# One full transpose a block for the router's scores, two normalisations and two joins moved to GpSimd, the last waits moved to SyncE

## What is computed

```python
n = layernorm(x)
s = sigmoid(silu(n @ s_w1.T + s_b1) @ s_w2.T + s_b2)
u = (n @ B_w.T + B_b) * s                  # 128 numbers a row
h[t] = h[t-1] @ A.T + u[t]                 # along each sequence
y = h @ C_w.T + C_b + n @ D_w.T + D_b
x1 = x + y * sigmoid(n @ g_w.T + g_b)
```

```python
n = layernorm(x1)
chosen = argmax(n @ gate_w.T)              # 8 scores a row
out = x1 + n + n @ expert_w[chosen].T
```

## Time and profile before

| | |
|---|---|
| median of 3 runs | 916.51 us |
| profiled execution | 915.37 us, of which span 913.6 us |
| PE busy | 894.5 us, 98% |
| DVE busy | 674.2 us, 74% |
| ACT busy | 651.8 us, 71% |
| POOL busy | 403.2 us, 44% |
| granted TensorE clock, mean over the span | 0.995 of full |
| a steady block (blocks 2 to 14) | 41.0 us |
| DMA | 172.36 MB, mean 189 GB/s |

### The profile page before, as it was taken

How to read it: one execution, slowest core, us unless ns; L and a number is a source line. 1 busy time by engine, 2 the same in 40 slices (tenths; PEclk the granted TensorE clock), 3 DMA queues, 4 the chain that set the end, 5 groups by cost and what they waited for, 6 DMA issues and landing times. The chain is left out here.

```text
span 913.6 us, 15779 instructions
## 1 busy us (share of the span) xinstructions
PE 894.5 (98%) x4461; PEld 722.8 (79%) x4462; DVE 674.2 (74%) x1697; ACT 651.8 (71%) x878; POOL 403.2 (44%) x640
## 2 busy tenths in 40 slices
PE   8999999999999999999999999999999999999995
PEld 7777878787878878787878878787877887888884
DVE  6777878788887878788787888787786465555552
ACT  5578697978879797978879797978534445666661
POOL 1033536281735536181735537181523453443442
PEclk9999999999999999999999999999999999999998
DMA  8445395867768495867668495867889879988871
GB/s 315 132 92 142 90 220 127 200 149 190 153 165 205 96 218 131 198 149 192 154 159 208 98 215 136 199 144 174 296 273 413 340 249 252 217 221 211 199 188 37
DMA packets 231049, 172.36 MB, mean 189 GB/s; under 512 B 155701, under 2 KB 189237, under 8 KB 229952
## 3 DMA queue, kind: packets, MB, share of 16 engines
q1 hardware_dynamic: 220032, 137.71, 60.5%
q0 software_dynamic: 10800, 33.70, 11.0%
q10 hardware_dynamic: 144, 0.07, 0.0%
HBM read 81.63 MB, written 54.68 MB: 149 GB/s over the span
## 5 line engine op out<-in xcount | busy, mean ns | idle before, releaser
L1757 PE MATMUL y<-experts,x1T_hi 128*128 x568 | 180.5, 399 | 0.8 <-DVE x1T_lo L1402 0.8
L597 POOL TENSOR_SCALAR ln_var_eps<-ln_mean_var 128x4 f32<-128x4 f32 x16 | 3.6, 224 | 277.0 <-DVE ln_mean_var L1078 276.9
L652 POOL DMA_INDIRECT out<-gate,ids x71 | 72.6, 1022 | 111.1 <-DVE gate L1421 78.6
L1757 PEld LDWEIGHTS y<-experts,x1T_hi 128*128 128x128 f32 x568 | 103.2, 188 | 20.8 <-issue 1.1
L1757 PE MATMUL y<-experts,x1T_lo 128*128 x284 | 111.5, 392 | 0.0
L587 POOL TENSOR_TENSOR y_biased<-y_biased,gate 128x256 f32<-128x256 f32 x120 | 93.3, 799 | 25.6 <-DVE y_biased L1068 25.5
L1456 PE MATMUL gates<-GwT_hi,xT_hi 128*128 128x512 f32 x256 | 104.0, 406 | 0.0
L1456 PE MATMUL y<-DwT_hi,xT_hi 128*128 128x512 f32 x256 | 102.6, 401 | 0.5 <-DVE gateT L1000 0.5
L1458 PE MATMUL gates<-GwT_hi,xT_lo 128*128 128x512 f32 x256 | 100.5, 393 | 0.0
L1421 DVE TENSOR_TENSOR gate<-y,raw_weights 128x512 f32<-128x512 f32 x71 | 49.0, 691 | 69.4 <-PE y L1757 63.8
L1457 PE MATMUL gates<-GwT_lo,xT_hi 128*128 128x512 f32 x256 | 100.2, 391 | 0.0
(11 more groups left out here) (283 smaller groups left out, 2328.9 us busy)
## 6 DMA issues: line engine op xcount, KB each, us to landing
raw_weights<-routed_rows SPq DMA_DIRECT2D x71, 258.0 KB, 3.2
x_in<-L_attn_x SPq DMA_DIRECT2D x32, 512.0 KB, 4.2
x_rows<-L_attn_x SPq DMA_DIRECT2D x32, 512.0 KB, 5.1
turned_experts<-raw_weights SPq DMA_DIRECT2D x32, 512.0 KB, 3.6
experts<-turned_experts SPq DMA_DIRECT2D x8, 2048.0 KB, 14.6
raw_weights<-L_ffn_expert_w SPq DMA_DIRECT2D x32, 256.0 KB, 3.1
routed_rows<-padrow SPq DMA_DIRECT2D x9, 258.0 KB, 4.6
out<-gate,ids POOLq DMA_INDIRECT x71, 3.9
```

The lines of the kernel that those rows point to most:

```text
L652: nc.gpsimd.indirect_dma_start(out=out_rows, out_offset=bass.IndirectOffsetOnAxis(ap=ids[r][:, 0:1], axis=0), in_=res[r], in_offset=None, ...
L1757: ins = nc.tensor.matmul(Y[m % 2][:], x2T[a][:, k, m % 2 * P:(m % 2 + 1) * P], flat[:, bass.ds(first + (w * KD + k) * D, D)], start=(k == ...
```

## The change

**Scores.** The tile scoresT becomes [128, 128], filled with zeros once. ScalarE copies each of the four tiles' [16, 128] to its own 32 partitions (two copies a pair, of 128 columns). One transpose of the whole tile, once a block, replaces four of 16 rows; it stands where the second turn-back stood, and the first one is gone. VectorE's sum skips the unused columns. Because the first turn-back no longer waits for ScalarE's first copy, the second pair's first score product does. **GpSimd** normalises tiles 3 and 4 of the next block (normalise_late) and joins both expert pieces of blocks 1 to 14 (join_piece); ScalarE keeps tiles 1 and 2 and the pieces of blocks 0 and 15, and waits for GpSimd's. **SyncE** holds the final waits for the output stores, which GpSimd held.

```diff
-    SC_RANK, SC_COUNT, SC_TURN = 2 * NT * E, 3 * NT * E, 2 * P
+    QUAD = P // NT
+    SC_RANK, SC_COUNT, SC_TURN = P, P + NT * E, 2 * P
...
-        scT = kb("scoresT", [2 * E, 2 * P])
+        scT = kb("scoresT", [P, P])
...  (sync, at its end)
+            for r in range(R):
+                sp.wait_ge(out_sent[r], 16 * len(range(r, SLOTS, R)))
...  (gpsimd, constants)
+                    nc.gpsimd.memset(scT[:], 0.0),
...
-                wait(pool, S_["xn_ready"], NT * b)
+                if b > 0:
+                    pool.wait_ge(S_["xn_ready"], NT + NT // 2 * (b - 1))
+                    wait(pool, S_["xn_late"], NT // 2 * (b - 1))
...
+            def normalise_late(b, i):
+                pool.wait_ge(S_["shift1_ready"], b + 1)
+                nc.gpsimd.tensor_scalar(xin[:, i, :], xin[:, i, :], rs1[:, i:i + 1], shift1[:, i:i + 1],
+                                        ALU.mult, ALU.add).then_inc(S_["xn_late"], 1)
+            def join_piece(b, j):
+                pool.wait_ge(w_flip[j], 16 * (b + 1))
+                pool.wait_ge(w_low[j], b)
+                nc.gpsimd.tensor_copy(planes(w_whole[j].rearrange("p k t -> p (k t)")),
+                                      w_flipped[j].rearrange("p (h k) t -> p h (k t)", h=2)).then_inc(w_joined[j], 1)
...  (gpsimd body, after the identities, before rstd2)
+                if b < LASTB:
+                    normalise_late(b + 1, 2)
+                    normalise_late(b + 1, 3)
+                if 0 < b < LASTB:
+                    for j in range(2):
+                        join_piece(b, j)
...  (gpsimd, at its end)
-            for r in range(R):
-                pool.wait_ge(out_sent[r], 16 * len(range(r, SLOTS, R)))
...  (scalar, scoresT)
-                nc.scalar.activation(scT[:], score_bank(b)[0:2 * E, SC_TURN:], ACT.Copy).then_inc(S_["scoresT_ready"], 1)
+                for i in range(2):
+                    at = (2 * pair + i) * QUAD
+                    ins = nc.scalar.activation(scT[at:at + 2 * E, :], score_bank(b)[0:2 * E, SC_TURN + i * P:SC_TURN + (i + 1) * P],
+                                               ACT.Copy)
+                ins.then_inc(S_["scoresT_ready"], 1)
...  (scalar, halve)
-                normalise1(b, i)
-                act.wait_ge(S_["xn_ready"], NT * b + i + 1)
+                if i < NT // 2:
+                    normalise1(b, i)
+                    act.wait_ge(S_["xn_ready"], NT + NT // 2 * (b - 1) + i + 1)
+                else:
+                    act.wait_ge(S_["xn_late"], NT // 2 * (b - 2) + i + 1)
...  (scalar, join_piece: the join itself only if b in (0, LASTB))
...  (tensor, score_product)
                 if n == 0:
                     pe.wait_ge(S_["x2T_lo"], NT * b + 2 * pair + 2)
+                    if pair > 0:
+                        counted_waits(pe, (S_["scoresT_ready"], 2 * b + pair))
...
-            def tail_back(b, pair):
-                counted_waits(pe, (S_["scoresT_ready"], 2 * b + pair + 1))
-                for i in range(2):
-                    at = (2 * pair + i) * 2 * E
-                    ins = nc.tensor.transpose(score_bank(b)[:, at:at + 2 * E], scT[:, i * P:(i + 1) * P], ident[0:2 * E, 0:2 * E])
-                ins.then_inc(S_["scores_psum"], 1)
+            def tail_back(b):
+                counted_waits(pe, (S_["scoresT_ready"], 2 * b + 2))
+                nc.tensor.transpose(score_bank(b)[:, 0:P], scT[:], ident[:]).then_inc(S_["scores_psum"], 1)
```

More of the change, by code:

```diff
@@ L185, in preln_ssm_moe_kernel @@
                      "bias_sum w_turned w_hi w_lo pow_psum pow_copied pow_hi pow_lo "
-                     "gate_stats gate_mean gate_centred stats1 mv1_ready ve1_ready rstd1_ready neg1_ready shift1_ready xn_ready xT_psum x_halves joined xT_hi xT_lo "
+                     "gate_stats gate_mean gate_centred stats1 mv1_ready ve1_ready rstd1_ready neg1_ready shift1_ready xn_ready xn_late xT_psum x_halves joined xT_hi xT_lo "
                      "s1_psum s1_sig silu_ready silu_hi silu_lo bt_psum s2_psum sel_ready "
@@ L549, in _ @@
                     nc.gpsimd.memset(xrow[0][:, :, D:RW], 0.0), nc.gpsimd.memset(xrow[1][:, :, D:RW], 0.0),
-                    nc.gpsimd.memset(zeros[:], 0.0), nc.gpsimd.memset(onehot[:, NT, :], 0.0), nc.gpsimd.memset(taken[:], 0.0)]
+                    nc.gpsimd.memset(zeros[:], 0.0), nc.gpsimd.memset(scT[:], 0.0), nc.gpsimd.memset(onehot[:, NT, :], 0.0), nc.gpsimd.memset(taken[:], 0.0)]
             for ins in made:
@@ L759, in join_piece @@
             def join_piece(b, j):
-                act.wait_ge(w_flip[j], 16 * (b + 1))
-                wait(act, w_low[j], b)
-                nc.scalar.activation(planes(w_whole[j].rearrange("p k t -> p (k t)")),
-                                     w_flipped[j].rearrange("p (h k) t -> p h (k t)", h=2), ACT.Copy
-                                     ).then_inc(w_joined[j], 1)
+                if b in (0, LASTB):
+                    act.wait_ge(w_flip[j], 16 * (b + 1))
+                    wait(act, w_low[j], b)
+                    nc.scalar.activation(planes(w_whole[j].rearrange("p k t -> p (k t)")),
+                                         w_flipped[j].rearrange("p (h k) t -> p h (k t)", h=2), ACT.Copy
+                                         ).then_inc(w_joined[j], 1)
                 act.wait_ge(w_joined[j], b + 1)
@@ L1088, in choose @@
             def choose(b):
-                dve.wait_ge(S_["scores_psum"], 2 * b + 2)
-                nc.vector.tensor_reduce(scores[:], score_bank(b)[:, 0:SC_RANK].rearrange("p (t h e) -> p t e h", h=2, e=E),
+                dve.wait_ge(S_["scores_psum"], b + 1)
+                parts = score_bank(b)[:, 0:SC_RANK].rearrange("p (t q) -> p t q", q=QUAD)[:, :, 0:2 * E]
+                nc.vector.tensor_reduce(scores[:], parts.rearrange("p t (h e) -> p t e h", e=E),
                                         AX.X, ALU.add).then_inc(S_["scores_ready"], 1)
@@ L1695, in body @@
                 gates(b, 1, 0, 1)
-                if tail:
-                    tail_back(b - 1, 0)
                 if not by_dma(b - 1, NT - 1):
@@ L1706, in body @@
                     if tail:
-                        tail_back(b - 1, 1)
+                        tail_back(b - 1)
                     over(b, 5)
@@ L1785, in last_tail @@
                     tail_scores(LASTB, 0)
-                elif s == 10:
-                    tail_back(LASTB, 0)
                 elif s == 11:
@@ L1790, in last_tail @@
                 elif s == 13:
-                    tail_back(LASTB, 1)
+                    tail_back(LASTB)
                 elif s == 15:
```

## The result

| | us, median | range | runs |
|---|---|---|---|
| before | 916.26 | 915.50 to 917.07 | 4 |
| after | 964.76 | 963.81 to 965.63 | 4 |

The ratio is 1.0529, 95% interval 1.0513 to 1.0544: 48.5 us more, where 8.6 us less was forecast, far outside the range of 904 to 913. The profiled execution after took 963.81 us with a span of 962.0.

A forecast was written before the change was run, and what follows sets the result against it. The prediction took TensorE's queue, busy 894.5 of 913.6 us, as the bound. Savings of 4.3 and 4.4 us at the two turn-backs, less 0.1 for a memset, gave 8.6 us: 907.9 us, range 904.0 to 913.0.

The forecast's parts named there:

- Part 1, the turn-back: Scores on TensorE: one full transpose a block replaces four small ones; 4.3 us saved at the second turn-back, 4.4 at the first.
- rival 4: TensorE's stall before the turn-back belongs to its wait, not its 16 rows, and stays: 912.2 us; chance 0.09.
- give-back: New TensorE wait for VectorE's last subtraction at a scan step the first turn-back had covered: 13 x 0.18 = 2.3 us lost.
- covered as below: ScalarE's scores copy of 0.37 us becomes two, 0.5 us taken; said to be hidden by ScalarE's lighter load.
- part 2: Normalisations and joins move from ScalarE to GpSimd: 0.7 and 1.3 us each, 18 us of room there, no gain alone.
- So this alone gains nothing.: Taking normalisations and joins off ScalarE saves no time, since TensorE never waits for ScalarE in a steady block.
- Rival 1: GpSimd's joined piece is late, ScalarE waits and TensorE loses 1.0 us in each of 13 blocks: 921 us; chance 0.09.
- No cost: GpSimd's first joined piece is ready at 415.4 us, ScalarE goes on as before: moving the work costs nothing.
- VectorE gets in its way: VectorE's operations slow GpSimd's new normalising and joining: 1 us added to GpSimd's stretch.
- Rival 2: GpSimd's new work slows VectorE's scan chain, 13 x 4 x 0.3 = 15.6 us more: 924 us; chance 0.09.
- Part 3: Last waits for the output stores move to SyncE: gain up to about 1 us, cost up to 0.5; 0 taken.
- scan subtractions above 0.4 us beside GpSimd's new work: Named sign, in VectorE's scan steps, that the forecast is wrong because GpSimd's work slows VectorE.

The follow-up runs named there:

- e17_relief: Kernel before with the full transpose; GpSimd normalises one column of tiles 3 and 4, ScalarE none of them: 907.82 us, 0.9906 of before.
- e1_scores: Kernel after with only the full transpose left; normalising, joins and last waits as before: 916.25 us, 0.9991 of before.
- e4_two_input: Kernel before with full transpose and late normalisations on GpSimd, each as two operations with two tensor inputs; no joins there: 929.70 us, 1.0148 of before.
- e5_gaps: Kernel after, with GpSimd waiting for the end of each of its four new operations: 924.95 us, 1.0082 of before.
- e16_dose: Kernel before, with two added back-to-back GpSimd copies whose results nobody uses: 931.63 us, 1.0167 of before.

## Why the prediction was wrong, step by step

1. *What bounds the kernel.* Right: TensorE, and the two turn-backs as its largest repeated stall.
2. *Part 1, the turn-back.* Right in size: 0.12 us measured for the full transpose (0.15 taken), the drain gone (rival 4 falls), a give-back of 2.4 us (2.3 taken) at the step that was named, and 8.6 us in all in e17_relief. Its own range was added up a little low: a transpose of 0.11 to 0.23 us and a give-back of 1 to 4 us make 906.0 to 910.9, not 905.5 to 910.5. But its condition was missed. The two score copies (0.53 us; 0.5 taken) were called "covered as below", and the cover is part 2. Without it they cost the whole gain (e1_scores).
3. *"So this alone gains nothing."* Wrong for that reason: taking ScalarE's work away was worth the difference between 916.25 and about 908 us.
4. *Part 2, durations and rooms.* Right: 0.78 us for a normalisation (0.7 taken), 1.32 for a join (1.3 taken), and GpSimd has room. Rival 1 was rightly small: ScalarE waits for the piece 7.1 us in all, and TensorE has no wait for the scores' copy.
5. *Part 2, "No cost".* This is the step that failed. It charged the contention to GpSimd: "VectorE gets in its way", with 1 us for GpSimd and nothing for VectorE. The earlier trace rows were read for a property of the kinds of operation, when they show an order of arrival, with 0.06 us between the two starts. The second pair in the same group, the indirect DMA beside the subtraction, had the other order and the other loser; e4_two_input and e5_gaps show the same loser wherever GpSimd had started first, and so did L1222 at 112.26 us in the trace that the prediction was made from.
6. *Rival 2.* The right mechanism at a chance of 0.09 and a price of 15.6 us. Its price rested on operations each delayed by 0.3 us. That is 1.2 us a block, with the clock untouched. What it left out is the queue: VectorE's operation waits for the rest of one GpSimd operation and for the joins behind it (up to 3.1 us), which cost TensorE 2.8 us of waiting a block, and the idle TensorE then had the lower clock for most of 4 us, another 1.7.
7. *Part 3.* Taken at 0, measured at -1.4 us; its bound was nearly right.

The signs that would show it wrong were named: "scan subtractions above 0.4 us beside GpSimd's new work". In every steady block the subtraction or the cast ahead of it lasted 2.0 to 3.2 us.

## What to carry to other kernels

Before work goes to GpSimd, list VectorE's operations from SBUF to SBUF that are on the path at that time, and charge each with the rest of the GpSimd operation that is running and, where copies are queued behind it without a wait, with these too. If such work must go there, let it wait for the VectorE operation behind which a gap comes: the same instructions took 965 us untimed and 909 timed. Where edits come together, ask of each whether another pays for its cover, as the relief of ScalarE did here for the transpose.

## What the runs showed of the hardware

- One operation of GpSimd that started first held VectorE's cast or SBUF subtraction to its end (0.77 us for 0.23). Two copies in a row held a cast for 2.27 us, and a normalisation with two copies behind it held VectorE for 3.1 us. Between two normalisations in a row it got in (cast 0.67 us, 9 of 9 times). A power of 4 columns (1.05 us) did not hold it (0.69 us). Started first, VectorE held GpSimd (1.89 us for 1.49). VectorE's additions with an input in PSUM were not held (0.30 us).
- After 2.53 us of idling TensorE ran at a granted clock of 0.61 over 4 us. With idle stretches of 0.54 us (e16_dose, the block shown) the mean clock was 0.996, and with stretches of up to 1.4 us (e5_gaps) 0.997.
- The span ended 6.4 to 6.5 us behind the end of the last store's issue when SyncE held the last waits (six traces) and 7.8 us when GpSimd did (eight).
